# Relative attention on one core: another order of the work inside a pair turn

## What is computed

```python
q, k, v = (qkv[0] * scale, qkv[1], qkv[2])
attn = jnp.einsum('bhid,bhjd->bhij', q, k)
qL = jnp.einsum('bhid,hdm->bhim', q, rpe_k_table)
attn = attn + jnp.take_along_axis(qL, idx, axis=-1)
kL = jnp.einsum('bhjd,hdm->bhjm', k * scale, rpe_q_table)
attn = attn + jnp.swapaxes(jnp.take_along_axis(kL, idx, axis=-1), 2, 3)
attn = jax.nn.softmax(attn, axis=-1)
out = jnp.einsum('bhij,bhjd->bhid', attn, v)
S = jax.vmap(lambda a, seg: jax.ops.segment_sum(a, seg, num_segments=NUM_BUCKETS))(a_t, rp)
out = out + jnp.einsum('inbh,hnd->bhid', S, rpe_v_table)
return x_out @ w_proj.T + b_proj
```

## Time and profile before

| | us |
|---|---|
| median of 3 runs | 2670.86 |
| lowest, highest | 2665.43, 2673.48 |
| the profiled execution | 2675.31 |
| its span in the profile | 2673.6 |
| granted clock, mean | 0.894 |
| relative attention in the trace, first to last maximum | 1546.9 to 2548.5 |

### The profile page before, as it was taken

One profiled execution on the slowest core, in us unless ns is written; L12 is line 12 of the kernel. 1 busy time (PEld: TensorE's weight loads), 2 busy tenths in 40 slices (PEclk: granted clock), 3 DMA queues, 4 the chain that ended last, 5 costly groups with the idle time before them and its releaser, 6 DMA issues. The chain is left out here.

```text
span 2673.6 us, 75473 instructions
## 1 busy us (share of the span) xinstructions
PE 2093.5 (78%) x32216; PEld 1301.3 (49%) x32216; DVE 1660.9 (62%) x2683; ACT 1226.2 (46%) x1845; POOL 508.5 (19%) x784
## 2 busy tenths in 40 slices
PE   1495888898886994288456389999999999999974
PEld 0263555556454563133255345555555555555533
DVE  5576445353534678444233378888888888888837
ACT  0374232313222774011133037776777677767744
POOL 0002000000000000300000054444444444444410
PEclk8697999998988996588777769999999999999986
DMA  3000000000000000101344855554554445545402
GB/s 96 1 1 24 17 3 17 2 17 3 1 18 2 1 1 5 28 23 39 146 95 96 210 143 129 142 141 129 136 129 129 126 129 132 144 119 141 114 21 67
DMA packets 326433, 195.07 MB, mean 73 GB/s; under 512 B 271376, under 2 KB 316126, under 8 KB 324830
## 3 DMA queue, kind: packets, MB, share of 16 engines
q1 hardware_dynamic: 315454, 139.68, 22.1%
q0 software_dynamic: 10240, 50.34, 5.0%
q10 hardware_dynamic: 416, 0.33, 0.0%
HBM read 91.69 MB, written 93.88 MB: 69 GB/s over the span
## 5 line engine op out<-in xcount | busy, mean ns | idle before, releaser
L1936 DVE TENSOR_REDUCE a1c_nm<-a1c_S 128x1 f32<-128x1024 f32 x512 | 609.3, 1217 | 113.2 <-PE a1c_S L2001 112.7
L1880 ACT ACTIVATE a1c_PT<-a1c_ST 128x1024 f32<-128x1024 f32 x512 | 523.0, 1022 | 68.6 <-PE a1c_ST L2001 65.8
L1895 ACT ACTIVATE a1c_Pb<-a1c_S,a1c_nm 128x192 f32<-128x192 f32 (+1 forms) x512 | 212.3, 415 | 216.8 <-DVE a1c_nm L1936 215.4
L1828 POOL TENSOR_TENSOR a1c_lt<-a1c_lt 128x256 f32<-128x256 f32 (+5 forms) x448 | 254.0, 567 | 35.5
L1926 DVE COPY a1c_PbT<-a1c_T 96x512 f32<-96x512 f32 x256 | 175.8, 687 | 99.3 <-PE a1c_T L2033 96.9
L2001 PE MATMUL a1c_S<-a1c_KR,a1c_Q 54*32 54x512 f16 (+13 forms) x2816 | 181.8, 317 | 21.8 <-DMA a1c_Gx<-a_bias 20.4
L2001 PE MATMUL a1c_ST<-a1c_Q,a1c_KR 57*128 57x256 f16 (+5 forms) x1088 | 180.4, 285 | 23.0 <-ACT a1c_PT L1880 21.1
L2001 PE MATMUL a1c_S<-a1c_KL,a1c_Q 54*32 54x512 f16 (+11 forms) x3136 | 193.4, 326 | 0.3
L2001 PE MATMUL a1c_S<-a1c_Gx,ident 64*32 64x96 f32 (+2 forms) x4352 | 185.9, 242 | 0.0
L2001 PE MATMUL a1c_ST<-a1c_Q,a1c_KL 57*128 57x128 f16 (+3 forms) x960 | 154.2, 267 | 25.0 <-ACT a1c_PT L1880 23.3
L2033 PE MATMUL a1c_T<-ident,a1c_Pb 128*96 128x128 f32 x1024 | 169.4, 289 | 0.8 <-DVE a1c_mhl L1950 0.8
(11 more groups left out here) (328 smaller groups left out, 4193.5 us busy)
## 6 DMA issues: line engine op xcount, KB each, us to landing
a_band<-a1c_Pb POOLq DMA_DIRECT2D x128, 384.0 KB, 3.4
a_bias<-a1b_G SPq DMA_DIRECT2D x32, 768.0 KB, 8.4
a1c_Gx<-a_bias SPq DMA_DIRECT2D x128, 192.0 KB, 4.4
a1c_Dt<-a_band SPq DMA_DIRECT2D x128, 126.0 KB, 3.5
a1c_Q<-a_qk SPq DMA_DIRECT2D x192, 64.0 KB
a1c_Vw<-a_values SPq DMA_DIRECT2D x64, 102.0 KB, 2.8
a1c_KL<-a_qk SPq DMA_DIRECT2D x96, 64.0 KB
a1c_KR<-a_qk SPq DMA_DIRECT2D x96, 64.0 KB
```

Source lines behind the costliest of these rows:

```text
L1828: add = lambda o, x, y: nc.gpsimd.tensor_tensor(o, x, y, ALU.add)
L1880: nc.scalar.activation(PT[:, q % 8, :, :], ST[:, :, :], ACT.Exp).then_inc(s["exp"], 1)
L1895: nc.scalar.activation(Pb[:, band_slot(I, c), w0:w1], SP[:, t % 2, I * P - 32 + w0:I * P - 32 + w1], ACT.Exp, bias=nm[:, t // 16 % 2, col: ...
L1936: nc.vector.tensor_reduce(nm[:, t // 16 % 2, col:col + 1], SP[:, t % 2, :], AX.X, ALU.max, negate=True).then_inc(s["max"], 1)
```

## The change

The order inside a pair turn is rewritten on three engines. TensorE: `turn`, query tile, `turn_band`, key unit, the band and diagonal share of the values (now a function of its own), query tile, values, key unit. ScalarE: `XOT`, `DT`, probabilities, band, probabilities, band. VectorE: moments, evacuation of `turn`, maximum, `band_out`, maximum. The waits follow: `turn_band(d)` now waits for the evacuation of the `turn` of the same pair turn (`last_turn_out(d + 1)`), `turn` for one band copy fewer, and the copy of `PV` for the last values.

```diff
@@ ScalarE
-            for d in range(LAST):
+            def outputs(d):
                 if d % 8 == 4 and 20 <= d < 20 + 8 * NHALF:
                     H = (d - 20) // 8
                     act.wait_ge(s["PVb"], ONE + 4 * H + 4)
+                    act.wait_ge(s["PV"], ONE + 8 * H + 8)
                     act.wait_ge(s["back"], ONE + H)
                     nc.scalar.activation(XOT[:, :], PV[:, :], ACT.Copy).then_inc(s["O_ev"], 1)
-                probabilities(2 * (d - JLAG))
+
+            def diagonals(d):
                 turn = turn_of(d)
                 if turn and turn[0] == "diag":
@@
+            for d in range(LAST):
+                outputs(d)
+                diagonals(d)
+                probabilities(2 * (d - JLAG))
                 band(2 * d)
                 probabilities(2 * (d - JLAG) + 1)
                 band(2 * d + 1)
@@ VectorE
             for d in range(LAST):
+                moments(d)
+                turn_out(d)
+                top(2 * d)
                 band_out(d)
-                moments(d)
-                top(2 * d)
-                turn_out(d)
                 top(2 * d + 1)
@@ TensorE
-                last_turn_out(d)
+                last_turn_out(d + 1)
@@ values, split in two
+            def band_values(d):
+                if place_of(d) is None:
+                    return
+                H, w = place_of(d)
@@
-                                     PbT[:, (8 * H + 2 * i + c // 2) % RING, at:at + P], False, w == 7)
+                                     PbT[:, (8 * H + 2 * i + c // 2) % RING, at:at + P], False, False)
@@ turn
-                pe.wait_ge(s["Tb_ev"], ONE + min(max(d - 1, 0), ND))
+                pe.wait_ge(s["Tb_ev"], ONE + min(max(d - 2, 0), ND))
@@
             for d in range(LAST):
+                turn(d)
+                by_query(2 * d)
                 turn_band(d)
                 by_key(2 * (d - JLAG))
-                by_query(2 * d)
+                band_values(d)
                 by_query(2 * d + 1)
-                turn(d)
+                values(d)
                 by_key(2 * (d - JLAG) + 1)
-                values(d)
```

More of the change, by code:

```diff
@@ L2105, in by_query, with place_of @@
                 ins.then_inc(s["S"], 1)
+            def place_of(d):
+                f = d - VLAG
+                H, w = divmod(f, 8)
+                return (H, w) if 0 <= f < ND else None
             def values(d):
-                f = d - VLAG
-                if not 0 <= f < ND:
+                if place_of(d) is None:
                     return
-                H, w = divmod(f, 8)
+                H, w = place_of(d)
                 n, qh = divmod(H, 2)
@@ L2130, in values @@
                 ins.then_inc(s["PV"], 1)
+            def band_values(d):
+                if place_of(d) is None:
+                    return
+                H, w = place_of(d)
+                n, qh = divmod(H, 2)
                 if w % 2 == 1:
```

## The result

| | before | after |
|---|---|---|
| median, us (runs) | 2672.17 (4) | 2789.80 (4) |
| lowest, highest | 2665.43, 2677.15 | 2774.56, 2791.98 |
| the profiled execution | 2675.31 | 2787.82 |
| its span | 2673.6 | 2786.1 |
| ratio, 95% interval | | 1.0432 [1.0406, 1.0459] |

The new order is slower by 4.3%. Forecast were 2772 us with a range of 2720 to 2815, and a chance of 0.87 for slower; on the profiled execution the forecast was +101 us, measured are +112.5.

A forecast was written before the change was run, and what follows sets the result against it. TensorE was taken to bound the kernel, with 1.7 us of stalls a half. Steady halves +84, tails +15 and the rest +2 gave +101 on 2675.3, 2776, adjusted to the median as 2772 us, range 2720 to 2815.

The forecast's parts named there:

- What bounds the kernel: TensorE in a half of 8 pair turns: 29.0 us of sections without stalls, 1.7 of stalls, against 30.72 measured.
- Stalls removed: TensorE: the 0.30 between key units and a second loop go; 0.12 newly lost in four pair turns, 0.5 a half.
- More changes of the array's form: TensorE: parted query tiles, and values parted from band share, cost +1.05 us a half, between 0 and 1.8.
- The shared bank: Band transposes wait for `T`: 0.9, 1.35, 0.35 us in pair turns 6, 4, 5; 0.2 plus 0.15 at 0.
- The half: Sum for 8 pair turns: 33.5 us against 30.72, +2.8; 84 us for 30 halves.
- Tails: Evacuation of tails holds TensorE: 12.3 us for a batch of 9, +15 for three batches.
- The rest: First 14 pair turns at clock 0.50: +2 us; after the last tile 0; shift and band transfers 0.
- The clock: Rival, much slower: TensorE's stalls bring pair turns 4 to 6 of every half to 1.2 GHz, 3100 us; chance 0.04.
- its mild form: Only a tenth of pair turns 4 to 6 fall to 1.2 GHz: 2805 us; the rival's chance is 0.04.
- What would show it: Signs: 16 pair turns about 67 us, band transposes wait 0.9, 1.35, 0.35; wrong if key units still wait 100 us.

The follow-up runs named there:

- the ScalarE order alone: Kernel before with ScalarE's second exponential moved ahead of its first band (probabilities, DT, probabilities, band, band), no other change: 2659.61 us, 0.9953.
- the last of the late band transposes: Kernel before with ScalarE's new order, band transposes behind the first key unit in pair turns 1 and 7, shift evacuated behind the second maximum: 2674.51 us, 1.0014.

## Why the prediction was right, point by point

- **What bounds the kernel.** 29.0 us of sections and 1.7 of stalls in a half. Right as far as it was tried: the ScalarE order alone took 0.6 of the 1.7 away, and the best kernel, with the late band transposes in pair turn 7, stands at 29.9 a half.
- **Stalls removed.** Right: matmuls' waits for exponentials fell from 44.4 to 7.5 us. The new one between second and first key unit, 0.12 by the sum, was 0.155 (band transposes to key unit 0.70 instead of 0.545); it is in the four pair turns that were named, and not in the 7.5.
- **More changes of the array's form.** Right in place, and in size for what was named: 0.50 for a parted tile, 0.98 for values ahead of a key unit. The sum was 1.05 a half and measured is 0.8 (29.8 less 29.0), because band transposes take 0.545 and not 0.57 in the new place.
- **The shared bank.** Right in all four places. The sizes were 1.49, 1.00, 0.47 and, as means over the halves, 0.32 + 0.32 against 1.35, 0.90, 0.35 and 0.2 + 0.15. The largest miss is the shift's, 0.3 over two waits. The term that was mis-sized in each of the five waits is the signal, by about 0.1: I took 0.05 us from the end of an evacuation to TensorE, by a row in which one engine waits for itself. From the end of `DT` (1972.12 + 0.61 = 1972.73) to the band transposes (1972.87) it is 0.14, and 0.15 from `xo` (1976.96 to 1977.11). That explains about 0.5 of the 0.65 by which the five together were too short; the rest stays open.
- **The half.** 33.5 forecast, 33.92 measured; before 30.72. 15 times twice the 0.42 is 12.6 us, more than the whole difference between +101 and +112.5. The 0.42 is itself a remainder: the waits at the bank were forecast 0.65 too short, those of the key units 0.1 too short and the sections 0.25 too long.
- **Tails.** Forecast 12.3 us a batch, measured 148.34 - 2 x 67.84 = 12.7. Right.
- **The rest.** Forecast 0 for the transfers. The kernel before takes 61.45 in its best stretches of 16 and up to 1.2 us more in others, 4.4 us over the nine without a tail; its key units and diag transposes wait for transfers 2.4 and 1.8 us, which is nearly that. In the kernel after no key unit waits for the shift's rows any more, and its waits for the transfer ahead of the diag transposes, 3.8 us in 5 waits, vanish behind the wait for `DT`: all its stretches without a tail take 67.85 but one, 68.23. So this step was off by 4 us to the other side. That it cancels the 3 us of the clock is luck.
- **The clock.** Called a rival with chance 0.04. It came, but smaller than its mild form of 2805: two falls, about 3 us together. The argument against it, a stretch at 2570 to 2580 with the clock at 1.00, did not hold here. With 0.6 us more of waiting in one pair turn of eight there were 31 falls.
- **What would show it.** One sign pointed wrong. "Key units still wait 100 us" was drawn from the weight loads' row, which rose to 185.7; the matmuls' row is the one that means lost time.

By the rule of the Trainium skill, page "TensorE: Matmul & The Clock Gate", section "Part 3: Packing small matmuls — row/col tiling", that the prediction weighed, parting values and band share would have cost nothing. The trace has values ahead of a key unit at 0.99 and 0.78, against 0.87 and 0.66 ahead of the band's share: the row had it right.

## What to carry to other kernels

Before moving a step that goes through a shared buffer, write down for both of its neighbours when the buffer is filled and when it is empty again, and follow the evacuation through the queue of the engine that makes it: here 0.60 us of copying cost up to 1.5 us because an exponential, a band and another copy stood ahead of it; moving it past the last two took half of the wait away. Stalls of an engine at 95% are worth only their own sum (1.7 of 30.7 us a half), while an order that avoids them can cost more in borders between array forms than it wins. The cheap edit was elsewhere, one exponential ahead of a band in ScalarE's queue, and showed only when the loop that goes round three engines was written out.

## What the runs showed of the hardware that was not expected

- The granted clock of TensorE fell from 1.00 to 0.50 in a phase in which TensorE was busy nine tenths of the time. The traces of four kernels have such falls there: 2 in the changed one (the first at 2108.98, 0.41 us after the start of band transposes that had waited 1.43), 31 and 23 with doubled copies, 2 in the last of the late band transposes. Each of the 58 lies behind a wait of TensorE of 1.3 us or more, or begins in it, and no kernel without such a wait had one. Such waits do not always bring a fall: the changed kernel has 25 of them and 2 falls, the doubled copies 58 and 31, 55 and 23, and the kernels with the turn put back and with all band transposes late have 1 and 3 and no fall. What in a stretch decides was not tried.
- A diagonal share followed by a query tile, both of 64 rows and 32 columns or fewer, run into each other: 0.94 us for both instead of 1.06.
- Evacuation to TensorE takes 0.14 to 0.15 us where band transposes follow, but 0.06 where a key unit does (2008.61, after an exponential that ran from 2007.53 to 2008.55 in the kernel before).
